# One core, a decoder layer: delta's thin products between the products that stack queries and keys

## The reference

```python
tau = sigmoid(conv1d(gelu(conv1d(x_conv, tau1_w, tau1_b, (1, 1), groups=D)), tau2_w, tau2_b, (0, 0)))
delta = sigmoid(conv1d(gelu(conv1d(x_conv, del1_w, del1_b, (1, 1), groups=D)), del2_w, del2_b, (0, 0)))
scores = einsum('bhqd,bhkd->bhqk', Q, K) / sqrt(DK)
scores = scores * tau[..., None] + delta[:, :, None, :]
attn = softmax(scores, axis=-1)
out = einsum('bhqk,bhkd->bhqd', attn, V)
```

## Time and profile before

| | |
|---|---|
| median of 3 runs | 329.12 us (328.66 to 329.18) |
| profiled execution | 331.18 us |
| its span | 329.4 us |
| mean granted TensorE clock | 0.974 |
| TensorE busy | 296.3 us, 90% |
| VectorE, ScalarE, GpSimd (POOL) busy | 270.4, 221.8, 170.3 us |

### The profile page before, as it was taken

One profiled execution on the slowest core, in us unless ns is written; L12 is line 12 of the kernel. 1 busy time (PEld: TensorE's weight loads), 2 busy tenths in 40 slices (PEclk: granted clock), 3 DMA queues, 4 the chain that ended last, 5 costly groups with the idle time before them and its releaser, 6 DMA issues.

```text
span 329.4 us, 6273 instructions
## 1 busy us (share of the span) xinstructions
PE 296.3 (90%) x1672; PEld 203.5 (62%) x1672; DVE 270.4 (82%) x566; ACT 221.8 (67%) x454; POOL 170.3 (52%) x248
## 2 busy tenths in 40 slices
PE   1999989599989999999979878888999999999995
PEld 1544965466555666566645756556777767777773
DVE  3895687388769887887985789999999889999994
ACT  8577638268794667566545776756677677777773
POOL 8002320000530087035067777676888888888893
PEclk9999877699999999999999999999999999999999
DMA  7700447867554120110005656457664667667721
GB/s 275 258 0 0 135 131 125 148 166 214 86 102 84 34 49 18 41 26 2 0 0 151 207 173 210 149 161 196 198 193 145 199 214 212 209 218 224 227 89 65
DMA packets 34540, 43.92 MB, mean 133 GB/s; under 512 B 5584, under 2 KB 22736, under 8 KB 34512
## 3 DMA queue, kind: packets, MB, share of 16 engines
q1 hardware_dynamic: 34512, 43.59, 47.0%
HBM read 34.92 MB, written 3.93 MB: 118 GB/s over the span
## 4 chain that ended last, share of the span: by engine, by line
PE 43%; POOL 18%; issue 10%; DVE 10%; DMA 8%; SPq 5%; ACT 3%; POOLq 0%; DVEq 0%; ACTq 0%
PE bank L442 31%; POOL qbd L1495 12%; POOL kst L1472 6%; DMA kbd<-kst 4%; DMA conv<-coefficient_rows 3%; PE bank L548 2%; PE bank L573 2%; SPq L395 2%; DMA pa<-pack_a 2%; DVE rawmax L1146 1%; PE bank L799 1%; DVE conv L1391 1%; PE bank L801 1%; PE bank L800 1%; PE bank L560 1%
## 5 line engine op out<-in xcount | busy, mean ns | idle before, releaser
L442 PE MATMUL bank<-khl,kst 128*128 128x512 f32 x396 | 105.9, 403 | 11.4 <-DVE kst L1183 9.3
L1495 POOL TENSOR_TENSOR qbd<-vs,qbd 128x512 fp32r<-128x512 f32 x65 | 84.3, 1298 | 30.4 <-ACT qbd L1027 30.1
L442 PEld LDWEIGHTS bank<-khl,kst 128*128 128x128 f32 x396 | 70.3, 188 | 39.5 <-DVE kst L1183 20.3
L997 ACT ACTIVATE bank<-bank 128x512 f32<-128x512 f32 x62 | 36.1, 582 | 33.9 <-PE bank L442 33.9
L1146 DVE TENSOR_REDUCE rawmax<-bank 128x4 f32<-128x512 f32 x64 | 43.0, 683 | 16.3 <-PE bank L442 15.3
L1027 ACT ACTIVATE qbd<-vs 128x512 fp32r<-128x512 f32 x66 | 41.1, 623 | 10.2 <-DVE vs L1400 5.8
L1391 DVE TENSOR_TENSOR conv<-bank,conv 128x512 f32<-128x512 f32 x61 | 41.7, 683 | 7.4 <-DMA conv<-coefficient_rows 4.9
L1183 DVE TENSOR_TENSOR kst<-ring,kst 128x256 fp32r<-128x256 f32 x62 | 46.7, 753 | 0.0
L1400 DVE TENSOR_TENSOR vs<-conv,bank 128x512 f32<-128x512 f32 x62 | 42.6, 687 | 3.2
L262 POOL TENSOR_SCALAR nwt<-mv 128x4 f32<-128x4 f32 x4 | 0.9, 228 | 77.3 <-DVE mv L1042 77.3
L442 PE MATMUL bank<-kbd,qst 128*128 128x512 f32 x64 | 35.0, 554 | 6.4 <-DMA kbd<-kst 5.1
(11 more groups left out here) (190 smaller groups left out, 475.7 us busy)
## 6 DMA issues: line engine op xcount, KB each, us to landing
conv<-coefficient_rows SPq DMA_DIRECT2D x122, 128.0 KB, 3.0
ring<-w SPq DMA_DIRECT2D x66, 192.0 KB, 2.9
kbd<-kst SPq DMA_DIRECT2D x60, 64.0 KB, 2.1
kst<-split_rows SPq DMA_DIRECT2D x12, 192.0 KB
split_rows<-khl SPq DMA_DIRECT2D x3, 512.0 KB, 3.6
split_rows<-khl SPq DMA_DIRECT2D x3, 256.0 KB, 2.3
split_rows<-qhl SPq DMA_DIRECT2D x3, 256.0 KB, 2.3
kst<-kst SPq DMA_DIRECT2D x12, 64.0 KB
```

Of the source, the lines that this page charges most:

```text
L442: return pe.matmul(out, lhsT, rhs, start=start, stop=stop)
L997: act.activation(out, four(2 + p), ACT.Silu).then_inc(silu_done, 1)
L1495: pool.tensor_tensor(hlo[:, k % 4, :].rearrange("p (b t) -> p b t", b=4), hx[k % 4], hhi[:, k % 4, :].bitcast(F32).rearrange("p (b t) -> p ...
```

## The change

The thin products of one batch are a function `delta(b)`. The loop over g calls it twice: for batch 2g behind the query stack and for batch 2g + 1 behind the key stack. The two waits that stood ahead of delta now stand ahead of the loop. Each batch signals `delta_done`, and VectorE waits for eight signals and not for one.

```diff
@@ -506,20 +506,23 @@
             pe.wait_ge(khi_ready, 2)
             pe.wait_ge(qlo_ready, 1)
             pe.wait_ge(klo_ready, 2)
+            pe.wait_ge(tau_ready, 2)
+            pe.wait_ge(gelu_done, 4)
+            d0 = cols_a["del2T"][0]
+            def delta(b):
+
+                for r in range(2):
+                    last = mm(bank[3][:, H * b:H * b + H], conv[:, 2 + r, b, :], pa[:, d0 + H * r:d0 + H * r + H],
+                              r == 0, r == 1)
+                last.then_inc(delta_done, 1)
+
             for g in range(G):
                 wait(pe, qst_ready, g - 1)
                 stack(bank[5 + g % 2], 0, qhl, 0, g, q_stacked)
+                delta(2 * g)
                 wait(pe, kst_ready, g - 1)
                 stack(bank[7 - 7 * (g % 2)], 2, khl[0], 0, g, k_stacked)
-
-            pe.wait_ge(tau_ready, 2)
-            pe.wait_ge(gelu_done, 4)
-            d0 = cols_a["del2T"][0]
-            for b in range(B):
-                for r in range(2):
-                    last = mm(bank[3][:, H * b:H * b + H], conv[:, 2 + r, b, :], pa[:, d0 + H * r:d0 + H * r + H],
-                              r == 0, r == 1)
-            last.then_inc(delta_done, 1)
+                delta(2 * g + 1)
@@ -1291,7 +1294,7 @@
             dve.wait_ge(rows_ready, 3)
             dve.wait_ge(ones_ready, 3)
-            dve.wait_ge(delta_done, 1)
+            dve.wait_ge(delta_done, B)
```

## The result

The changed kernel is slower: a median of 331.49 us (331.10 to 331.64, 4 runs) against 328.89 us (328.61 to 329.18), ratio 1.0075 with a 95% interval of 1.006 to 1.009. That is +2.6 us where +0.7 was forecast, and it lies above the range.

What follows compares the result with a forecast made beforehand. Bound by a chain from TensorE's products through SyncE's DMA issues to TensorE's restart. Seven batches (3.0 us) less 1.75 cover gave +1.25, less 0.57 given back: +0.68, from 329.12 to 329.8 us, range 328.9 to 331.0.

Steps and rivals of the forecast that it cites:

- The reading of the path: TensorE's loop has no gap, so seven delta batches at 0.43 us delay the last key stack by 3.0 us.
- The rival of more hidden loads: In the loop, wide products hide more of a batch's four weight loads; net -0.15 to +0.27 us, chance 0.15.
- the free batches: In the loop, batches fill time TensorE would spend waiting for copies; net -0.95 us, 328.2 us, chance 0.05.
- a clock that falls within the loop: The level falls half way through the stack loop: +4.35 us, less at most 2.0; 331.5 to 333.5 us, chance 0.06.
- a restart that finds the full level: TensorE's restart after its pause runs at full clock, so 2.38 us of loss vanish; 328.0 us, chance 0.08.
- the two moved waits: Ahead of TensorE's loop, the waits for gelu_done and tau_ready cost nothing, being signalled before queries already waited for.
- the delay of +1.25 us: Fourth score product ends later, so SyncE's copies for batch 2 start at 45.22 us instead of 43.97.
- the 1.75 us of cover: Delta products behind the stack loop cover copies there; delay is 7x - 1.75 us for a batch of x us.
- The half level for that product: The fourth score product runs at half clock because TensorE was idle just before: 0.63 us against 0.40 at full.
- SyncE's own order doesn't add to it: SyncE's batch 1 copies and three row stores finish at 44.4 us, before the copies due at 45.2.
- What comes back: The clock rise stays at 66.53 us, so a later restart spends 1.25 us less at half level: -0.57 us.
- nothing comes back: Rival: the clock rise moves with the restart; +1.25 us, 330.4 us, or 330.8 with a 0.49 us batch; chance 0.20.

Runs made afterwards that it cites:

- Experiment 7: Changed kernel with all eight batches of delta ahead of the stack loop, not between its products; 332.92 us, ratio 1.0107 to the kernel before.
- experiment 2: Kernel before with only the two waits (tau_ready, gelu_done) moved ahead of the loop, delta left behind it; 328.13 us, ratio 0.9997.
- experiment 5: Delta late: five batches behind the loop, three behind the fourth score product, VectorE's maxima of batch 0 before the delta sum; 327.44 us, ratio 0.9957 to the kernel before.
- experiment 6: As experiment 5, but all eight batches of delta behind the fourth score product; 328.49 us, ratio 0.9985 to the kernel before.
- Experiment 8: Only batch 0 of delta made, behind the loop, the other seven left out and VectorE waiting for one signal; 328.96 us, ratio 1.0007 to the kernel before.
- Experiment 10: Kernel before with SyncE alone waiting for the second half's queries ahead of its copies for step 1; 330.43 us, ratio 1.0044.
- experiment 11: Kernel before, unchanged, for a third profile; copies for batch 2 at 42.67 us, restart at 59.14, span 327.9 us.
- experiment 12: Kernel before, unchanged, for a fourth profile; copies for batch 2 at 43.32 us, restart at 60.03, span 326.5 us.
- experiment 1: Kernel before, unchanged, run again with a profile of another execution; 328.73 us over 12 runs, ratio 0.9998, profiled span 326.7 us.
- experiment 4: Changed kernel, unchanged, run again with a profile of another execution; 331.33 us over 11 runs, ratio 1.0085 to the kernel before.
- experiment 3: Changed kernel with batches 0 to 3 of delta each behind a key stack, batches 4 to 7 behind the loop; 329.29 us, ratio 1.0034 to the kernel before.
- the shared runs of experiments 1 to 12: Runs of the kernel before, shared by experiments 1 to 4, 5 to 8 and 9 to 12; medians 328.81, 328.79 and 328.58 us.

## Why the prediction was wrong

**The reading of the path was right.** All added work fell on the path of the last key stack. A batch cost (39.25 - 32.84 - 3.29) / 7 = 0.446 us (forecast 0.43); the loop ran at 0.92 us for a stack and a batch (forecast 0.89); the idle time ahead of the scores was 1.99 us (nearly 2); `edelta` stood right behind `low_queries`, so the seven more signals were not late. Experiment 7 shows that a batch has the same price without the alternation. The rival of more hidden loads is refuted, since a batch paid all four of its loads (4 x 0.108 = 0.43 us). Of the two readings of the Trainium skill's rule (TensorE: Matmul & The Clock Gate, "Step-by-step: what each phase is for") the 0.446 us agree with one load ahead, not with a deep run of them. Refuted are also the free batches, a clock that falls within the loop (granted 1.0 from 32 to 42 us; it did fall there in the profile of experiment 7), and a restart that finds the full level (granted 0.5 from about 60.2 to 66.9 us).

**The terms that were short.** The loop started 0.38 us later than in the profile before. Of that, 0.21 us is the price of the two moved waits (experiment 2), a term that the prediction put at nothing because their signals come early; they do, and the waits still take time. The other 0.17 us is a difference between executions: the products ahead of the loop start that much later, and four profiles of before spread over 0.4 us there. Seven batches took 0.1 us more, and the first score product came 0.26 us after ScalarE's last copy, a price of waking that the sum didn't have: 42.31 for 41.5. On the path through VectorE the maxima began at 43.55 (forecast 43.20), the fourth score product at 44.88 (44.53), the copies for batch 2 at 45.75 (45.22). So the sum for the changed kernel was right to 0.5 us.

**The step that failed: the delay of +1.25 us, taken against the fourth score product of one execution, and the 1.75 us of cover that came from it.** In that execution the clock was half from 39.22 to 46.05, just where the score products and values of batch 0 lie. So SyncE's copies went out at 43.97, later than in any other profile of before. With the full level the same order has them at 42.38 (experiment 2). The changed kernel depends on the level far less: its fourth score product waits for ScalarE's and VectorE's copies and for the second maximum, so only its own length changes, 0.63 us for 0.40. It started at 44.88 and 45.01 in the two profiles, both with the half level from about 43 us on; none caught it at the full level there. The delay is therefore 1.8 us against the shown execution, 2.4 us in the mean and 3.4 us against an execution with the full clock. In the means, the start of SyncE's queue moved by 3.5 us (37.3 to 40.8), and 1.1 us of it were covered, not 1.75.

The half level for that product came in as forecast, but by luck: the prediction took it "because TensorE was idle just before", and TensorE went on at the full level after its pause (granted 0.99 from 42 to 43 us) and lost it only at work.

Beneath it lay a limit that the prediction dismissed with "SyncE's own order doesn't add to it". It checked the queue of the changed kernel against the late fourth score product, and never that of before against an early one. The queue needs 4.44 us from the completed key stacks on; from 37.4 us that is 41.8. Where the row stores issue more slowly (experiments 5, 6 and 8) it needs 4.9 to 5.4 us, up to 42.98. Started at 40.76 it can't be there before 45.2. Experiment 10 measured a late queue alone at +1.4 to +1.9 us. In the changed kernel both limits moved together, the queue to 45.2 and the score product to 45.75; by these numbers an earlier score product alone would win back 0.5 us there, which was not tried.

**"What comes back", -0.57 us, failed as well.** It held the changes of the clock level to the times that one profile had. They lie elsewhere in each execution: in the first five lines of the table the first fall behind 38 us came at about 39.2, 39.5, 40.8, 40.8 and 48.3 us, and the last rise ahead of 70 us at 66.5, 63.4, 64.7, 64.7 and 65.4. Over many executions nothing that can be told is given back: the loss in the runs, +2.6 us, is no smaller than the delay of the copies. The nearest of the rivals was "nothing comes back", for 330.4 to 330.8 us: right in that, and short by 0.7 us for the reason above. With +2.4 us for the +1.25 and nothing for the -0.57, the prediction's sum gives +2.4 us, against +0.68 forecast and +2.6 measured.

**What hid the result in the profiles.** The shown execution of before lost a further 0.4 to 1 us between SyncE's copies and the restart (17.3 us, against 16.3 to 16.9 in the other lines of the table). The profiled pair differs by 0.8 us at the restart, and by -0.17 at the first score product of step 8 (99.01 and 98.84): ahead of step 7 before waited 0.82 us for a key copy by DMA, the changed kernel didn't. This is not that one execution alone: experiments 11 and 12 waited 0.99 and 0.46 us there, experiments 1, 2 and 4 not at all. So what lies behind the restart does not move rigidly, as the prediction had it, and a profile of before can lose there what it was ahead. Median and profiled time of before stood 2.06 us apart on the page. The prediction named that number and carried it over as a constant between a profiled and a timed execution. It was the sign that this execution is not the usual one: of 104 timed executions of before only two took longer than its 331.18 us.

**Open.** Experiment 8 (less work, earlier copies, no gain) is explained for its profiled execution alone, and experiment 3 (whose interval holds two theories) is not settled. Nor is what makes the three row stores take 1.94, 2.51 and 2.22 us to issue in experiments 5, 6 and 8, where the score products start near 39 us, and at most 1.54 us in the eleven other profiles. Why the key copy of step 7 is late in some executions isn't known either.

## What to carry to other kernels

Thin products behind a loop can be the cover of the copies that end it; put between the loop's products they cost their full time, as many of them as stand ahead of the last stack that others wait for. Before a delay is summed, ask for each engine that starts from that stack how long its own queue is, the DMA issues above all, and work it out for the fast case of the kernel before, too. When the profiled time lies as far from the median as here (0.6%), take more profiles before using one: its clock dips and late transfers need not be terms of the sum. And a wait whose signal has long come isn't free: two of them took 0.21 us of TensorE's time here.

## What the runs showed of the hardware

Much of the spread goes with the clock level. In 104 timed executions of the kernel before (the shared runs of experiments 1 to 12 and experiment 1 itself) the mean time rises as the mean granted clock falls:

```
mean clock of the execution   executions   mean us
0.988 to 0.990                 9           327.31
0.983 to 0.984                34           327.97
0.977 to 0.979                30           328.85
0.972 to 0.974                13           329.30
0.967 to 0.969                18           330.23
```

By this the first four runs of before, within 0.6 us, gave too narrow a picture: 104 of them reach from 325.7 to 332.0.

One execution of experiment 7 took 387.16 us at a mean granted clock of 0.735; the other eleven took 329.64 to 334.74.

After its pause of 2 us TensorE worked on at the full level in the changed kernel, and the level fell only a little later. Its stretches: us, busy (instructions), granted clock, DMA share, GB/s.

```profile
38.00:40.00 2.00, 2.00 (x16) 1.00 0.00 0
40.00:42.00 2.00, 0.32 (x3) 1.00 0.00 0
42.00:43.00 1.00, 0.69 (x4) 0.99 0.43 89
43.00:46.00 3.00, 3.00 (x14) 0.50 0.76 233
```
